# A routed mixture-of-experts layer behind attention: new opening and closing orders, and 18 idle products on TensorE

## The chip, the cores and the metric

The kernel runs on 1 core of one Trainium2 chip. The metric is device time in microseconds (us) of one launch. The engines are named as in the profile: PE is TensorE, DVE is VectorE, ACT is ScalarE, POOL is GpSimd, SP is the engine that issues most DMAs.

## The reference

Two residual blocks over x of shape (2, 1024, 128), in fp32:

```python
# attention with one latent for queries and keys
xn = layernorm(x)
latent = xn @ W_basis.T                        # 64 wide
v = xn @ W_v.T + b_v
scores = latent @ latent.T / sqrt(64)          # causal, within a batch
y = softmax(scores) @ v                        # same weights for all heads
x = x + layernorm(y @ W_o.T + b_o)
# 64 experts of 88 rows, top 8 of the best 4 of 8 groups, plus 2 shared ones
xn = layernorm(x)
s = sigmoid(xn @ gate_w.T); choice = s + gate_bias
group_score = sum of the two largest of each group of 8
masked = choice where the group is among the best 4, else 0
w = s at top8(masked); w = w / (sum(w) + 1e-20) * 2.5
routed = sum_e w[e] * (silu(xn @ Wg[e].T) * (xn @ Wu[e].T)) @ Wd[e].T
x = x + layernorm(routed + shared_mlp(xn))
```

## The kernel before

**Tiles.** The 2048 tokens are 16 tiles of 128 and four quarters ("quads") q of 512. Every expert product is one of 512 columns, and to keep fp32 accuracy each is done as three products of fp32r parts: high by high, high by low, low by high (`products`, lines 1303 to 1305). The weights of 16 experts by 8 rows make one chunk of 128 rows; there are 11 rounds of 4 chunks ("sets") c. A step is one chunk for one quad: gate and up (6 products), ACT's Silu (`gate`), DVE's up times route weight (`weigh`, line 1005) and gate times up (`hidden`, line 1015), ACT's high part (`hidden_hi`), POOL's low part (`hidden_lo`), and the down products (3) three steps later, which add up in one PSUM bank per quad.

**Order.** Each engine has its own program, and semaphores tie them. The steps of the first round and all of attention and routing are mixed by hand-written lists, `PE_ORDER`, `ACT_ORDER`, `DVE_ORDER` and `POOL_ORDER`; the last round and the output norm go by `PE_TAIL`, `ACT_TAIL`, `DVE_TAIL`, `POOL_TAIL`. Between them run plain loops over the rounds. An engine works through its list strictly in order: a stage that waits holds up all that stand behind it.

**Stages of the opening.** S statistics of x and P its norm and transposition (quad 0 on DVE, the others on POOL, `norm_x`); Q the latent product and its split into `lat_hi`, `lat_lo` and a scaled copy `lat_hl`; B on DVE the centring of W_o and b_o, B on POOL the making of `sel`, a matrix that copies a routing weight to its chunk's rows; K the product of W_v and W_o; V the values; A score rows and exponentials; T their transposition; C the weighted values; D, U, X, Y the attention's norm and the next one; E the transposed expert input, F the logits, H, J, I, O, M the routing (groups, experts, scores, sum of weights and `route`), G the transposition of `route`, N its spreading over the chunks (`route_w`), L and R the splits of shared and routed weights. Z is gate and up of a step, W its hidden parts and, on PE, the down products of the step two before.

Before anything else PE does ten products of 128x128 identities, and nothing reads them (line 1377).

**Stages of the closing.** D k is the down product of step k-3. The last quad is done in two halves of 256 columns. T k on PE multiplies finished columns by `center` (I - 1/128), which transposes them and takes their mean off; S k and N k on DVE are its statistics and the scaling and residual (line 1122), Y k the reciprocal root: on POOL for units 0 to 3, and for the last, unit 4, on ACT (Sqrt, line 839) with a DVE reciprocal. O copies a finished bank to `y_t`; O3 on ACT copies the last quad's bank, and O4 on DVE (line 1099) adds the second half's bank to it, after the last down products and ahead of T4. W20 on DVE makes the last low part.

Of the kernel before, what the change touches and what calls it, by code (L numbers as in the profile page):

```python
# [1499 lines left out]
```

## Time and profile before

| | |
|---|---|
| time, median of 3 runs | 477.61 us (476.32 to 477.9) |
| the profiled execution's own time | 477.6 us |
| its span, from the first to the last instruction | 475.6 us |
| PE busy | 455.8 us (96%) |
| DVE busy | 325.5 us (68%) |
| POOL busy | 335.9 us (71%) |
| ACT busy | 286.0 us (60%) |
| mean granted TensorE clock | 0.983 |

Busy times are modelled for PE, whose products overlap, so the spacing of their starts tells more than the duration of one. The granted clock is a share of full speed: 1.00 is 2.4 GHz, 0.50 is 1.2 GHz. All times in the rows count from the span's start.

### The profile page before, as it was taken

Reading aid. Unit: us, or ns where it says so; the run is one execution under the profiler, and the core shown is the slowest. Engines: PE = TensorE matmul, PEld = TensorE weight load, DVE = VectorE, ACT = ScalarE, POOL = GpSimd, SP = SyncE. Lnnn points to the kernel's source line nnn. Section 1 sums busy time; section 2 is a strip of 40 time slices with the busy share of each in tenths; the row PEclk is TensorE's granted clock in tenths of the full one; section 3 lists DMA queues with packets and bytes.
Section 4 is the critical chain, followed back from the end, with each engine's and each line's share of the span. In section 5 each row is a group of like instructions: output and inputs, shape, how many; then the busy total and the mean of one; then the engine's idle time right before and its main releaser. Section 6 shows DMA issues by size and latency. Waiting matters only on the chain.

```text
span 475.6 us, 8043 instructions
## 1 busy us (share of the span) xinstructions
PE 455.8 (96%) x2152; PEld 370.5 (78%) x2152; DVE 325.5 (68%) x694; ACT 286.0 (60%) x573; POOL 335.9 (71%) x318
## 2 busy tenths in 40 slices
PE   6999986999999999999999999999999999999995
PEld 4889774767778888888888888888888888888894
DVE  5666989786466666666666666666666666666786
ACT  2577985855665565565556555555655555566563
POOL 6853667765677767777776777777677777768674
PEclk8899997999999999999999999999999999999999
DMA  7000000000010100001010000101000010100002
GB/s 180 25 3 2 18 17 19 17 1 0 1 51 19 34 17 20 31 17 33 17 33 17 23 26 17 33 17 33 17 22 28 17 33 17 33 0 0 0 23 67
DMA packets 12856, 11.58 MB, mean 24 GB/s; under 512 B 2549, under 2 KB 12837, under 8 KB 12837
## 3 DMA queue, kind: packets, MB, share of 16 engines
q1 hardware_dynamic: 11973, 11.02, 8.0%
q10 hardware_dynamic: 864, 0.33, 0.4%
q8 instruction: 9, 0.15, 0.1%
q14 instruction: 10, 0.08, 0.1%
HBM read 10.30 MB, written 1.05 MB: 24 GB/s over the span
## 4 chain that ended last, share of the span: by engine, by line
PE 89%; ACT 5%; DVE 2%; issue 2%; DMA 1%; ACTq 0%; POOL 0%; DVEq 0%
PE ps L1303 27%; PE ps L1305 26%; PE ps L1304 26%; PE ps L1255 2%; PE ps L1243 1%; PE ps L1203 1%; PE ps L1274 1%; PE ps L1298 1%; PE ps L1195 1%; PE ps L1223 1%; PE ps L1224 1%; PE ps L1454 1%; DMA bv_sb<-in_b_v 1%; ACT xn L672 1%; ACT exp_t L712 1%
## 5 line engine op out<-in xcount | busy, mean ns | idle before, releaser
L547 POOL TENSOR_TENSOR lat_hi<-hid,lat_hl 128x512 fp32r<-128x512 f32 (+1 forms) x187 | 239.9, 1285 | 101.5 <-ACT lat_hl L768 97.1
L754 ACT ACTIVATE ps<-ps 128x512 f32<-128x512 f32 (+1 forms) x180 | 103.1, 573 | 132.1 <-PE ps L1305 131.8
L1005 DVE TENSOR_TENSOR up_w<-ps,route_w 128x512 f32<-128x512 f32 (+1 forms) x180 | 122.2, 679 | 85.2 <-PE ps L1305 84.7
L1015 DVE TENSOR_TENSOR hid<-ps,up_w 128x512 f32<-128x512 f32 (+1 forms) x180 | 122.4, 680 | 33.6 <-DVE up_w L1005 28.3
L1303 PE MATMUL ps<-x_hi,w_hi 128*128 128x512 f32 (+1 forms) x360 | 141.2, 392 | 2.8 <-ACT route_w L740 2.4
L1305 PE MATMUL ps<-x_hi,w_lo 128*128 128x512 f32 (+1 forms) x360 | 140.5, 390 | 0.0
L1304 PE MATMUL ps<-x_lo,w_hi 128*128 128x512 f32 (+1 forms) x360 | 140.2, 389 | 0.0
L768 ACT CAST lat_hl<-hid 128x512 fp32r<-128x512 f32 (+1 forms) x188 | 113.4, 605 | 14.2 <-DVE hid L1015 11.7
L1303 PEld LDWEIGHTS ps<-x_hi,w_hi 128*128 128x128 f32 x360 | 68.0, 189 | 19.4 <-issue 4.3
L1305 PEld LDWEIGHTS ps<-x_hi,w_lo 128*128 128x128 f32 x360 | 68.1, 189 | 15.0
L1304 PEld LDWEIGHTS ps<-x_lo,w_hi 128*128 128x128 f32 x360 | 68.0, 189 | 14.5
L1303 PE MATMUL ps<-lat_hl,w_hi 128*128 128x512 f32 (+1 forms) x180 | 71.4, 397 | 0.5 <-POOL lat_hi L547 0.5
L1305 PE MATMUL ps<-lat_hl,w_lo 128*128 128x512 f32 (+1 forms) x180 | 69.7, 387 | 0.0
L1304 PE MATMUL ps<-lat_hi,w_hi 128*128 128x512 f32 (+1 forms) x180 | 69.2, 385 | 0.0
L555 POOL TENSOR_TENSOR w_lo<-w_raw,w_hi 128x384 fp32r<-128x384 f32 x44 | 45.0, 1024 | 3.1 <-ACT w_hi L748 3.1
L1303 PEld LDWEIGHTS ps<-lat_hl,w_hi 128*128 128x128 f32 x180 | 33.8, 188 | 8.4 <-POOL lat_hi L547 1.2
L1305 PEld LDWEIGHTS ps<-lat_hl,w_lo 128*128 128x128 f32 x180 | 33.7, 187 | 8.1
L1304 PEld LDWEIGHTS ps<-lat_hi,w_hi 128*128 128x128 f32 x180 | 33.8, 188 | 7.2
L748 ACT CAST w_hi<-w_raw 128x384 fp32r<-128x384 f32 x44 | 22.6, 517 | 4.9 <-PE ps L1305 4.9
L895 DVE TENSOR_REDUCE neg_max<-ps 128x1 f32<-128x128 f32 (+7 forms) x16 | 12.0, 752 | 11.1 <-PE ps L1225 11.0
L1255 PE MATMUL ps<-vals,exp_t 128*128 128x129 f32 x144 | 18.3, 278 | 0.6 <-ACT att L693 0.4
L1255 PEld LDWEIGHTS ps<-vals,exp_t 128*128 128x128 f32 x144 | 17.1, 191 | 1.4 <-issue 1.2
(140 smaller groups left out, 366.9 us busy)
## 6 DMA issues: line engine op xcount, KB each, us to landing
w_raw<-in_w_experts SPq DMA_DIRECT2D x44, 192.0 KB, 2.4
x_sb<-in_x SPq DMA_DIRECT2D x3, 256.0 KB, 4.9
out<-x_sb SPq DMA_DIRECT2D x3, 256.0 KB, 2.3
x_sb<-in_x ACTq DMA_DIRECT2D x2, 64.0 KB, 2.3
x_sb<-in_x SPq DMA_DIRECT2D x2, 64.0 KB, 2.1
out<-x_sb SPq DMA_DIRECT2D x1, 128.0 KB, 1.8
out<-x_sb SPq DMA_DIRECT2D x2, 64.0 KB, 1.6
sh_raw<-in_w_shared_up SPq DMA_DIRECT2D x1, 88.0 KB
```

Of the source, the lines that this page charges most:

```text
L547: g.tensor_tensor(hid_lo[:, k % DEEP, 0:w], hid[:, k % 2, 0:w], hid_hi[:, k % DEEP, 0:w], ALU.subtract).then_inc(s_hlo, 1)
L555: g.tensor_tensor(w_lo[:, c, :], w_raw[:, c, :], w_hi[:, c, :], ALU.subtract).then_inc(s_wlo, 1)
L748: a.copy(w_hi[:, c, :], w_raw[:, c, :]).then_inc(s_whi, 1)
L754: a.activation(bank, bank, ACT.Silu).then_inc(s_gated, 1)
L768: a.copy(hid_hi[:, k % DEEP, 0:w], hid[:, k % 2, 0:w]).then_inc(s_hhi, 1)
L895: v.tensor_reduce(neg_max[:, k:k + 1], rows.rearrange("p a b -> p (a b)")[:, 0:width], AX.X, ALU.max, negate=True).then_inc(s_max, 1)
L1005: v.tensor_tensor(up_w[:, k % 2, 0:w], ps[:, gate_bank(k) + 1, 0:w], route_w[:, group, 512 * q + lo:512 * q + lo + w], ALU.mult).then_inc( ...
L1015: v.tensor_tensor(hid[:, k % 2, 0:w], ps[:, gate_bank(k), 0:w], up_w[:, k % 2, 0:w], ALU.mult).then_inc(s_hid, 1)
L1255: mm = t_.matmul(ps[:, 7, 256 * (r % 2):256 * (r % 2) + C + 1], exp_t[:, r % 2, j, :], vals[:, (q // QPB) * TPB + j, 0:C + 1], start=(j == 0),
L1303: t_.matmul(out_, hi, mhi, start=start, stop=False)
L1304: t_.matmul(out_, hi, mlo, start=False, stop=False)
L1305: return t_.matmul(out_, lo, mhi, start=False, stop=stop)
```

## The change

- **Opening norm.** The reciprocal root of quad 0 leaves POOL: ACT takes a Sqrt, DVE a reciprocal, and each normalised tile is signalled by itself. Two small activations (Sqrt, Exp) are placed to bring their tables in.
- **Latent.** `lat_hi` is signalled before its scaled copy, which is now read from `lat_hi`.
- **Routing weights.** One small DVE operation per quad is gone: the 2.5 stands in `sel`, the 1e-20 in a 65th column of `left`.
- **Idle products.** A stage I on PE: 2, 6 and 10 products of 512 columns into a bank that the next user overwrites. Line 1377's ten become eight, and one more follows P0.
- **Closing.** The down weights of the last chunk are centred beforehand (stage C: three DVE operations, one ACT copy, one POOL subtraction), and the last down product is done as six products of 128 columns that add to T4's bank; T3 and T4 stand before it. The last two units' variances come from ACT (Square with a running sum, then Sqrt), not from DVE's statistics and POOL's power.
- **Orders.** All eight lists are rewritten.
- **Buffers.** `wc` and `wc_hi` stand where `left` stood and are together as large; the other new ones and `left` stand behind all the rest. `deviation` is twice as long.

```diff
-        deviation = sb("deviation", [P, 4])
+        deviation = sb("deviation", [P, 2, 4])
-        left = sb("left", [P, 4, E])
+        wc = sb("wc", [P, C])
+        wc_hi = sb("wc_hi", [P, C], F32R)
...
+        first_dev = sb("first_dev", [P, 6])
+        y_var = sb("y_var", [P, 2, 2])
+        wc_stats = sb("wc_stats", [P, 6])
+        wc_mean = sb("wc_mean", [P, 2])
+        left = sb("left", [P, 4, E + 1])
+        wc_lo = sb("wc_lo", [P, C], F32R)
...
         PE_ORDER = stages(
-            "P0 Q0 K0 V0 A00 P1 A01 A02 Q1 T00 T02 A03 C00 C01 T04 T06 A10 C02 C03 A11 P2 V1 "
...
-            "E1 T34 F1 T35 W1 C31 G0 T36 T37 Z0 C32 N00 C33 Z1 E2 F2 Z2 N01 G1 Z3 W2 Z4 W3 Z5 "
+            "P0 Q0 K0 A00 V0 P1 A01 A02 T00 Q1 A03 T02 C00 C01 T04 T06 A10 C02 C03 A11 P2 T10 "
...
+            "E1 T34 F1 T35 C31 T36 G0 Z0 W0 T37 C32 N00 C33 Z1 E2 F2 N01 Z2 I0 G1 I1 Z3 W1 I2 "
+            "W2 Z4 W3 Z5 E3 W4 Z6 N10 F3 N11 W5 G2 Z7 W6 W7 N20 Z8 Z9 W8 W9 N21 Z10 Z11 Z12 "
...
         ACT_ORDER = stages(
-            "R2 T37 Z0 N00 Y2 C33 Z1 E2 R3 F2 G1 W0 N01 W1 Z2 W2 Z3 Z4 Y3 W3 Z5 W4 E3 Z6 W5 "
+            "G0 T36 T37 Y2 N00 C33 Z1 E2 F2 G1 Z2 N01 W0 W1 Z3 W2 R3 Y3 W3 Z4 Z5 W4 E3 Z6 W5 "
...
         DVE_ORDER = stages(
-            "S0 B0 P0 S1 S2 B1 Q0 A00 A01 A02 K0 V0 A03 Q1 S3 A10 A11 A12 V1 U0 A13 Q2 X0 V2 "
-            "A20 A21 Q3 A22 A23 U1 F0 A30 X1 V3 H0 A31 A32 J0 I0 O0 M0 A33 U2 F1 X2 H1 G0 J1 "
-            "Z0 I1 O1 Z1 U3 F2 M1 H2 J2 X3 Z2 I2 Z3 G1 Z4 O2 Z5 M2 Z6 F3 G2 Z7 H3 Z8 Z9 J3 Z10 "
+            "S0 P0 S1 B0 B1 Q0 K0 A00 V0 A01 A02 S2 A03 Q1 A10 S3 A11 A12 V1 A13 U0 Q2 A20 X0 "
+            "V2 A21 Q3 A22 A23 U1 V3 X1 A30 F0 A31 H0 A32 J0 I0 O0 U2 M0 A33 X2 F1 H1 G0 J1 Z0 "
+            "I1 O1 Z1 U3 M1 F2 H2 J2 X3 Z2 I2 Z3 G1 Z4 Z5 O2 M2 Z6 F3 G2 Z7 H3 Z8 Z9 J3 Z10 "
...
         POOL_ORDER = stages(
-            "S0 S1 P1 B0 S2 P2 D0 S3 P3 X0 D1 F0 X1 L0 J0 D2 E0 R0 M0 F1 R1 X2 E1 L1 J1 D3 E2 "
-            "F2 M1 W0 R2 J2 W1 X3 R3 W2 W3 W4 M2 F3 W5 W6 E3 W7 W8 J3 W9 W10 W11 W12 M3 W13 "
+            "B0 S1 P1 S2 P2 S3 D0 P3 X0 R0 D1 R1 R2 F0 X1 L0 L1 E0 J0 D2 M0 F1 X2 J1 E1 D3 F2 "
+            "M1 E2 J2 W0 X3 W1 R3 W2 W3 W4 E3 M2 W5 F3 W6 W7 W8 W9 J3 W10 W11 W12 M3 W13 W14 "
...
         PE_TAIL = stages(
-            "D11 Z13 D12 Z14 D13 Z15 D14 Z16 D15 Z17 T2 D16 D17 D18 Z18 T3 Z19 D19 D20 D21 D22 "
-            "T4 "
+            "D11 Z13 D12 Z14 D13 Z15 D14 Z16 Z17 D15 T2 Z18 D16 D17 D18 Z19 D19 D20 D21 T3 T4 "
+            "D22 "
...
         ACT_TAIL = stages(
-            "W11 Z11 Z12 W12 W13 Z13 Z14 W14 Z15 O2 Z16 W15 W16 Z17 O3 W17 W18 Z18 Z19 W19 W20 "
-            "Y4 P0 "
+            "O1 W11 Z11 Z12 W12 Z13 W13 Z14 W14 W15 Z15 O2 Z16 Z17 W16 W17 Z18 W18 W19 Z19 O3 "
+            "W20 Y3 Y4 P0 "
...
         DVE_TAIL = stages(
-            "Z19 W20 S3 O4 N2 S4 N3 N4 "
+            "S2 Z19 O4 W20 N2 N3 N4 "
...
+        FILLS = (2, 6, 10, )
...
                     link(g.affine_select(out=sel_f[:], in_=sel_f[:], compare_op=ALU.not_equal,
-                                         fill=1.0, base=base, channel_multiplier=1,
+                                         fill=ROUTED_SCALE, base=base, channel_multiplier=1,
...
+                elif what == "C":
+                    pool.wait_ge(s_wchi, 1)
+                    g.tensor_tensor(wc_lo[:], wc[:], wc_hi[:], ALU.subtract).then_inc(s_wclo, 1)
...
-            a.copy(lat_hi[:, own], ps[:, 1, :])
-            a.activation(lat_hl[0:R, own], ps[0:R, 1, :], ACT.Identity,
-                         scale=SCALE).then_inc(s_lhi, 1)
+            a.copy(lat_hi[:, own], ps[:, 1, :]).then_inc(s_lhi, 1)
+            act.wait_ge(s_lhi, q + 1)
+            a.activation(lat_hl[0:R, own], lat_hi[0:R, own], ACT.Identity,
+                         scale=SCALE).then_inc(s_lhs, 1)
...
             for n in range(2, 4):
                 a.dma_start(x_sb[:, n, :], x_tiles[:, n, :]).then_inc(s_x0[n], 16)
+            act.wait_ge(s_eps, 1)
+            a.activation(first_dev[:, 4:5], eps_col[:], ACT.Sqrt)
             a.dma_start(wv_sb[:], w_v).then_inc(s_wvl, 16)
             a.dma_start(wo_sb[:], w_o_t).then_inc(s_wvl, 16)
             a.dma_start(bv_sb[:], b_v).then_inc(s_wvl, 16)
             a.dma_start(bo_sb[:], b_o.to_broadcast([P, C])).then_inc(s_bol, 16)
+            act.wait_ge(s_var, 1)
+            a.activation(first_dev[:, 0:4], mv[:, 0, :, 1], ACT.Sqrt,
+                         bias=eps_col[:]).then_inc(s_dev0, 1)
+            a.activation(first_dev[:, 5:6], eps_col[:], ACT.Exp)
...
                 elif what == "Y":
-                    act.wait_ge(s_var, len(VARIANCES) + k + 1)
-                    a.activation(deviation[:, 0:2], mv[:, 2 + k % 2, 0:2, 1], ACT.Sqrt,
+                    act.wait_ge(s_yp, k + 1)
+                    for t in range(UNITS[k][2]):
+                        ins = a.activation(squares[:, t, 0:C], ps[:, unit_bank(k), P * t:P * t + P],
+                                           ACT.Square, scale=float(C) ** -0.5,
+                                           accum_out=y_var[:, k % 2, t:t + 1])
+                    ins.then_inc(s_yvar, 1)
+                    act.wait_ge(s_yvar, k - len(UNITS) + 3)
+                    a.activation(deviation[:, k % 2, 0:2], y_var[:, k % 2], ACT.Sqrt,
                                  bias=eps_col[:]).then_inc(s_dev, 1)
...
+            def norm_x0():
+                dve.wait_ge(s_dev0, 1)
+                v.reciprocal(rstd[:, 0], first_dev[:, 0:4]).then_inc(s_rstd, 1)
+                dve.wait_ge(s_rstd, 1)
+                for t in range(4):
+                    ins = v.tensor_scalar(xn[:, 0, t, :], x_sb[:, t, :], mv[:, 0, t, 0:1],
+                                          rstd[:, 0, t:t + 1], ALU.subtract, ALU.mult)
+                    ins.then_inc(s_xn0, 1)
...
                 link(v.tensor_reduce(wsum[:], left[:], AX.X, ALU.add))
-                link(v.tensor_scalar(wsum[:], wsum[:], 1e-20, 1.0 / ROUTED_SCALE, ALU.add,
-                                     ALU.mult))
                 v.reciprocal(winv[:], wsum[:]).then_inc(s_winv, 1)
...
+                elif what == "C":
+
+                    dve.wait_ge(s_wl[SETS - 1], 16 * ROUNDS)
+                    rows = w_raw[:, SETS - 1, WD:WD + P]
+                    link(v.bn_stats(wc_stats[:], rows))
+                    link(v.bn_aggr(wc_mean[:], wc_stats[:]))
+                    v.tensor_scalar(wc[:], rows, wc_mean[:, 0:1], None,
+                                    ALU.subtract).then_inc(s_wc, 1)
                 elif what == "O":
 
-                    dve.wait_ge(s_down, LAST_S + unit_step(k) + 1)
+                    dve.wait_ge(s_down, LAST_S + unit_step(k))
...
+                pe.wait_ge(s_lhs, q + 1)
                 pe.wait_ge(s_llo, q + 1)
...
+            def last_down(k):
+
+                pe.wait_ge(s_wclo, 1)
+                pe.wait_ge(s_hlast, 1)
+                for t in range(2):
+                    own = slice(P * t, P * t + P)
+                    to = ps[:, unit_bank(len(UNITS) - 1), own]
+                    hi, lo = hid_hi[:, k % DEEP, own], hid_lo[:, k % DEEP, own]
+                    t_.matmul(to, hi, wc_hi[:], start=False, stop=False, skip_group_check=True)
+                    t_.matmul(to, hi, wc_lo[:], start=False, stop=False, skip_group_check=True)
+                    mm = t_.matmul(to, lo, wc_hi[:], start=False, stop=True,
+                                   skip_group_check=True)
+                mm.then_inc(s_yp, 1)
+
+            def fill_wait(k):
+
+                pe.wait_ge(s_eta, turns_through(4 * QUADS))
+                for _ in range(FILLS[k]):
+                    t_.matmul(ps[:, acc_bank(0), :], ident_r[:], x_hi[:, 0:512], start=True, stop=True)
...
-            for _ in range(10):
-                t_.matmul(ps[:, 6, 0:P], ident[:], ident[:], start=True, stop=True)
+            def keep_busy(n):
+                for _ in range(n):
+                    t_.matmul(ps[:, 6, 0:P], ident[:], ident[:], start=True, stop=True)
+
+            keep_busy(8)
             for at, (what, q, n) in enumerate(PE_ORDER):
                 if what == "P":
                     turn_xn(q, at)
+                    if q == 0:
+                        keep_busy(1)
```

## Rows read from the trace of the kernel before

**Rows 1.** Busy time in stretches: us, each engine's busy us (instructions), granted clock, DMA.
```profile
0.00:66.54 66.54, 59.73 (x400) 51.83 (x400) 46.44 (x182) 46.77 (x120) 40.17 (x67) 0.95 0.17 44
66.54:81.00 14.46, 9.01 (x35) 6.92 (x36) 12.57 (x54) 7.29 (x18) 10.15 (x11) 0.76 0.06 15
74.00:88.00 14.00, 11.64 (x42) 8.69 (x43) 13.09 (x49) 10.26 (x21) 10.89 (x13) 0.76 0.10 29
...
110.00:430.00 320.00, 319.31 (x1382) 257.81 (x1381) 210.87 (x306) 188.04 (x349) 234.03 (x192) 1.00 0.08 22
```

**Rows 2.** Whom TensorE waited for, 64 to 120: us, times, longest.
```profile
PE ps L1303 <- ACT route_w L740: 2.4, 1, 2.4
PE ps L1283 <- POOL route L575: 1.7, 1, 1.7
```

**Rows 3.** The same busy-time columns in half microseconds, around the clock's falls and rises.
```profile
9.00:9.50 0.50, 0.47 (x1) 0.32 (x2) 0.47 (x3) 0.00 (x0) 0.42 (x2) 0.75 0.97 217
...
16.00:16.50 0.50, 0.50 (x5) 0.50 (x4) 0.20 (x1) 0.50 (x2) 0.50 (x1) 0.92 0.00 0
...
74.00:74.50 0.50, 0.00 (x0) 0.00 (x0) 0.48 (x1) 0.50 (x2) 0.00 (x0) 0.60 0.00 0
...
80.50:81.00 0.50, 0.50 (x2) 0.36 (x2) 0.50 (x1) 0.00 (x0) 0.35 (x2) 0.57 0.00 0
```

**Rows 4.** Chain that ended last, one piece at low clock: start, us, what.
```profile
77.84 0.43 PE ps L1303
```

**Rows 5.** Timeline of the opening: start, us, engine, line, operation [idle before].
```profile
3.64 1.28 ACT L659 ACT_TABLE_LOAD   x1 [3.64 <-issue]
3.97 0.38 DVE L867 BATCH_NORM_AGGREGATE mv<-stats 128x2 f32<-128x6 f32 x4
...
5.78 0.29 DVE L987 BATCH_NORM_STATS2 wo_stats<-wo_sb 128x6 f32<-128x128 f32 x1 [1.44 <-DMA bv_sb<-in_b_v]
...
6.53 1.11 DVE L876 TENSOR_SCALAR xn<-x_sb,mv,rstd 128x128 f32<-128x128 f32 x4
...
9.03 1.89 PE L1195 MATMUL ps<-xn_t,wb_sb 128*128 128x512 f32 x2 [0.68 <-ACT xn_t L659]
...
10.46 3.41 POOL L565 TENSOR_SCALAR xn<-x_sb,mv,rstd 128x128 f32<-128x128 f32 x4
...
12.32 2.05 PE L1203 MATMUL ps<-wvo_sb,xn_t 128*128 128x128 f32 x8 [0.55 <-ACT wvo_sb L783]
```

**Rows 6.** Timeline from the second quarter's routing to the first routed step.
```profile
71.28 0.48 DVE L979 TENSOR_SCALAR wsum<-wsum 128x4 f32<-128x4 f32 x1
...
72.04 1.04 POOL L575 TENSOR_TENSOR route<-left,winv 128x512 f32<-128x512 f32 x1 [0.32 <-DVE winv L981]
...
74.89 1.08 ACT L740 COPY route_w<-ps 128x512 f32<-128x512 f32 x2
...
81.08 0.69 DVE L1015 TENSOR_TENSOR hid<-ps,up_w 128x512 f32<-128x512 f32 x1
```

**Rows 7.** Timeline of the last ten microseconds.
```profile
465.31 0.59 ACT L843 COPY y_t<-ps 128x512 f32<-128x512 f32 x1 [1.92 <-PE ps L1305]
...
468.81 1.28 ACT L839 ACT_TABLE_LOAD   x1
468.83 0.42 DVE L1105 TENSOR_TENSOR lat_hi<-hid,lat_hl 128x256 fp32r<-128x256 f32 x1 [0.47 <-ACT lat_hl L768]
...
469.97 0.42 DVE L1099 TENSOR_TENSOR y_t<-ps,y_t 128x256 f32<-128x256 f32 x1
...
470.45 0.71 PE L1454 MATMUL ps<-center,y_t 128*128 128x128 f32 x4 [0.52 <-DVE y_t L1099]
...
472.15 0.30 ACT L839 ACTIVATE deviation<-mv,eps_col 128x2 f32<-128x2 f32 x1 [2.05 <-DVE mv L867]
...
472.75 0.61 DVE L1122 SCALAR_TENSOR_TENSOR x_sb<-ps,rstd,x_sb 128x128 f32<-128x128 f32 x2
```

**Rows 8.** Instructions of line 690: ns min/median/max, first and last start.
```profile
L690 ACT ACTIVATE squares<-ps x16: 271/280/287, 20.7 to 66.5; 128x129 f32<-128x129 f32 x16
```

More of the change, by code:

```diff
@@ L318, in stage_before @@
             return found[-1] if found else None
-        NORMS = [st[:2] for st in POOL_ORDER if st[0] in "SDX"]
+        NORMS = [("S", 0)] + [st[:2] for st in POOL_ORDER if st[0] in "SDX"]
         VARIANCES = [st[:2] for st in DVE_ORDER if st[0] in "SX"]
@@ L483, in _ @@
             g.memset(minus_half[:], -0.5)
+            g.memset(left[:, :, E:E + 1], 1e-20)
             g.memset(eps_col[:], EPS).then_inc(s_eps, 1)
@@ L574, in write_route @@
                     pool.wait_ge(s_rtp, q)
-                g.tensor_tensor(route[:], left[:].unsqueeze(2).to_broadcast([P, 4, 2, E]),
+                g.tensor_tensor(route[:], left[:, :, 0:E].unsqueeze(2).to_broadcast([P, 4, 2, E]),
                                 winv[:, :].unsqueeze(2).unsqueeze(3).to_broadcast([P, 4, 2, E]),
@@ L835, in _ @@
                     act.wait_ge(s_eps, 1)
-                    a.activation(deviation[:, 2:3], eps_col[:], ACT.Sqrt)
+                    a.activation(deviation[:, 0, 2:3], eps_col[:], ACT.Sqrt)
                 elif what == "Y":
-                    act.wait_ge(s_var, len(VARIANCES) + k + 1)
-                    a.activation(deviation[:, 0:2], mv[:, 2 + k % 2, 0:2, 1], ACT.Sqrt,
+                    act.wait_ge(s_yp, k + 1)
[6 more added lines that the diff above has]
+                    a.activation(deviation[:, k % 2, 0:2], y_var[:, k % 2], ACT.Sqrt,
                                  bias=eps_col[:]).then_inc(s_dev, 1)
+                elif what == "C":
+                    act.wait_ge(s_wc, 1)
+                    a.copy(wc_hi[:], wc[:]).then_inc(s_wchi, 1)
                 elif what == "O":
@@ L870, in _ @@
             made = [0]
-            def scale(n, k, src, dst):
-                dve.wait_ge(s_rstd, n + 1)
-                for t in range(4):
-                    ins = v.tensor_scalar(dst(t), src(t), mv[:, k, t, 0:1], rstd[:, k, t:t + 1],
-                                          ALU.subtract, ALU.mult)
-                return ins
             def flat(t3):
@@ L965, in choose_experts @@
                 for t in range(4):
-                    ins = v.match_replace(left[:, t, :], top8[:, t, :], masked[:, t, :], TAKEN)
+                    ins = v.match_replace(left[:, t, 0:E], top8[:, t, :], masked[:, t, :], TAKEN)
                 link(ins)
@@ L972, in pick_scores @@
                     dve.wait_ge(s_route, q)
-                v.scalar_tensor_tensor(out=left[:], in0=left[:], scalar=TAKEN, in1=scores[:, q % 2],
-                                       op0=ALU.is_equal, op1=ALU.mult).then_inc(s_picked, 1)
+                v.scalar_tensor_tensor(out=left[:, :, 0:E], in0=left[:, :, 0:E], scalar=TAKEN,
+                                       in1=scores[:, q % 2], op0=ALU.is_equal, op1=ALU.mult).then_inc(s_picked, 1)
             def sum_weights(q):
@@ L1114, in _ @@
                     q, first, n = UNITS[k]
-                    if k + 1 == len(UNITS):
+                    if k + 2 >= len(UNITS):
                         dve.wait_ge(s_rstd, len(NORMS) + k)
-                        dve.wait_ge(s_dev, 1)
-                        v.reciprocal(rstd[:, 2 + k % 2, 0:n], deviation[:, 0:n]).then_inc(s_rstd, 1)
+                        dve.wait_ge(s_dev, k - len(UNITS) + 3)
+                        v.reciprocal(rstd[:, 2 + k % 2, 0:n],
+                                     deviation[:, k % 2, 0:n]).then_inc(s_rstd, 1)
                     dve.wait_ge(s_rstd, len(NORMS) + k + 1)
@@ L1404, in _ @@
                     logits(q, at)
+                elif what == "I":
+                    fill_wait(q)
                 elif what == "Z":
@@ L1443, in _ @@
                         down(kd, LAST_S + kd, q, w_hi[:, c, :], w_lo[:, c, :], P,
-                             start=(lo > 0 and c == 0), stop=(c == SETS - 1), lo=lo, w=w)
+                             start=(lo > 0 and c == 0),
+                             stop=(c == SETS - (2 if lo else 1)), lo=lo, w=w)
                 elif what == "T":
@@ L1455, in _ @@
                                        y_t[:, q, P * (first + t):P * (first + t) + P], center[:],
-                                       start=True, stop=True, skip_group_check=True)
-                    mm.then_inc(s_yp, 1)
+                                       start=k + 1 < len(UNITS) or t == 0, stop=True,
+                                       skip_group_check=True)
+                    if k + 1 < len(UNITS):
+                        mm.then_inc(s_yp, 1)
 def kernel(L0_attn_hidden_states, L0_attn_W_basis, L0_attn_W_v, L0_attn_b_v, L0_attn_W_o,
```

42 lines of the change are left out of this document (26 added, 16 removed), and 23 rows, old and new, of tables (ACT_ORDER, DVE_ORDER, PE_ORDER, POOL_ORDER).

## The prediction

> **What bounds the kernel now.** I read the page's shares first: PE 96% busy, DVE 68%, POOL 71%. That is a mean, so the next view is the busy time by stretches [rows 1]. From 110 to 430 us, PE is busy for 319.3 of 320 us with 1382 products, one every 0.231 us: the loops are PE's, and no edit touches them. What can be won lies in the 110 us before and the last 12 us. The reader is to see there three kinds of loss.
>
> First, PE stands still or starts late in the opening: the first latent product starts at 9.03 us [rows 5]. Second, between 66.5 and 81 us PE is busy for only 9.0 of 14.5 us [rows 1]; the view of who waited for whom puts 1.7 us on POOL's `route` and 2.4 us on ACT's `route_w` [rows 2]. Third, the granted clock: it falls at 9.25 us and is back at 16.0, and falls at 74.1 and is back at 80.9 (the shares 0.75, 0.92, 0.60 and 0.57 of half-microsecond windows give the points) [rows 3]. Both stretches last 6.8 us at 0.50, which is 1.2 GHz. Before each, PE had been doing short work with gaps. In the second a product takes 0.43 us instead of 0.231 [rows 4]. PE works in it from 76.2 (its wait ends just behind the copies at 75.97 [rows 6]) to 80.9, so 4.7 us of time did what takes half: 2.35 us lost, at most.
>
> At the end, PE's last products end at 471.16 us and the span at 475.6: a chain of statistics, root, scaling and a DMA.
>
> **The opening.** Before: statistics ready at 3.97 + 0.38 = 4.35; DVE then waits for the weights (until 5.76) for the centring, and norms only at 6.53 to 7.64; PE transposes from 7.70, ACT copies, and the latent product starts at 9.03 [rows 5]. Now P0 stands ahead of the centring. ACT has issued its last DMA at 3.6. The new Sqrt table load comes right behind the first two DMA issues. If it lies beside the other four, Sqrt runs at 4.4, 0.30 long [rows 7], the reciprocal ends at about 4.9, and the tiles are ready by 6.05 (1.11 as in [rows 5]). Eight idle products end there too. Transposition ends near 6.5, the copy 0.6 later, the latent product starts at 7.2: 1.8 us earlier. If the load holds the issues up by its 1.28 us plus an activation, all is 0.5 later (gain 1.3) and W_o, the value weights and b_o land 1.5 us later. DVE's Q0 now stands behind B1, which waits for b_o; that can eat another 0.7 or so. The Exp load, 1.28 [rows 5], lies from 4.7 to 6.0, under the norm. It costs nothing while the transposition ends after 6.1, and up to 0.5 us when it doesn't.
>
> What follows? V0 ran from 12.32 to 14.37, with A00 and P1 behind it [rows 5], so P1 came no earlier than 14.7. Now A00 goes as soon as the split is done, near 10.1, and V0 behind it. P1 needs POOL's norm of quad 1 (3.41 long, ending at 13.87 [rows 5]). POOL makes `sel` first now and then starts it when DVE's statistics, which stand behind P0, are there: 7.3 + 1.5 + 3.4 = 12.2. So PE idles a little before P1 again, and the gain there is 14.7 - 12.3 = 2.4 at most. If the clock falls as before, V0 costs 2.05 again [rows 5] and P1 comes 1 us earlier or less. From 16 to 66 us PE is nearly gapless and ACT runs close to full in places, so what is won is carried but not increased. I take 1.8 us; bounds 0.3 (issues late, clock fallen, b_o late) and 3.5 (no low stretch over dense work: half of 1.89 and of 2.05 back, plus the earlier start).
>
> The two loads here are priced by the profile: 1.28 us each, at both places where one is seen [rows 5, 7]. What the trace cannot show is the rest of a switch, because both of its loads end in a long wait. The Trainium skill (ScalarE: Activation LUTs, section What ACT_TABLE_LOAD costs) gives 2.66 us for every switch of set, a drain being part of it; by that the opening's sum would be 1.0 us instead of 1.8, an estimate from that page. I go by the trace, and the dearer switch is a rival below.
>
> **The middle.** The DVE operation that is gone took 0.48 us for quad 1 [rows 6]. M1 is also moved ahead of F2 on DVE. On POOL, F2 still stands ahead of M1, but E2 (x's low part) now comes behind M1. `route` started at 72.04 and would start at 71.45, 0.6 earlier; so does G1 on PE. Z3 doesn't wait for G1 itself. It waits for ACT's two `route_w` copies (1.08 us [rows 6]), which stand behind G1 on ACT, and now behind Z2's Silu too, which I price as ACT's copy of 512 columns, 0.59 [rows 7]; of the 0.6 little is left if PE is late with it, but Z2's product is long done. So Z3, which waited until the copies ended at 75.97, starts some 0.5 us earlier, near 75.7 against 76.2: the waits stay. Into them go the idle products: 2 before G1 (0.46 us; in a wait that was 1.7 us and is now 1.1), 6 before Z3 (1.39, in one that was 2.4 [rows 2]), and 10 before the first down product (2.31). PE's longest pause shrinks from 2.4 to about 1.2 us, so I expect the second low stretch to be gone, +2.35 us.
>
> The last ten are covered only in part. The down product needs POOL's low part of step 0, which needs ACT's W0, now behind N01, and on POOL stands behind E2 and J2: about 78.3. Z3 at full clock ends at 77.1 and the ten at 79.4: 1.1 us too many. Without their cover all ten would cost 2.3.
>
> And PE cannot cash in everything: DVE is busy for 13.09 of the 14 us from 74 to 88 [rows 1], with routing and step work mixed. Z5 needs step 3's `hidden`, which ended at 81.77 [rows 6], 0.8 us after the clock was back. DVE has 0.9 us of idle time in those 14 us, and gains the removed operation, 0.48; so with DVE behind it PE can come about 1.4 us earlier. The sum by PE is 0.5 + 2.35 - 1.1 = 1.75. I take 1.5 us, between the two; bounds -1 (fills late, DVE order worse) and 3.5.
>
> **The closing.** ACT's O3 waited 1.92 us for the last quad's down products [rows 7] with two high parts queued behind it; these delay POOL, and so steps 18 and 19. Now O3 stands behind Z19, and Z18 stands three down products earlier (1.05 us). W20's part on DVE started at 468.83; its input would be there near 467.6 by the 1.05 us and what O3 no longer holds up. Then O3 (0.59), O4 (0.42) and the low part (0.42) follow on ACT and DVE: about 468.6. PE: T3 behind D21 and O3, T4 behind O4, end near 468.7; last product, six of 128 columns, about 0.65: 469.4.
>
> Then the price. ACT's Y3 does two squares (0.28 each [rows 8]; with their sums read I take 0.75 for two, up from 0.56), and only then needs Sqrt's table. Before, the load ran at 468.81, hidden in a wait of 2 us [rows 7]. Now it stands between Y3's squares and its root, and Y4 queues behind it: 468.25 + 0.75 + 1.28 + 0.3 = 470.6, squares to 471.35, root 471.7, reciprocal 471.9, scaling 0.61: 472.5 against 473.36 [rows 7]. Gain 0.8 us; bounds -0.6 (the shortening above fails, the load stays) and 2.1 (the load is hidden). Stage C adds 0.8 us to DVE, 0.3 to ACT and 0.4 to POOL in a stretch where PE is the bound; two DVE statistics and one POOL root go. I cost it at nothing; if DVE were late there, 0.8.
>
> **The sum.** 1.8 + 1.5 + 0.8 = 4.1 us. The profiled execution took 477.6 us with 2.0 outside its span, and its time is the median of the runs shown. So 477.6 - 4.1 = 473.5 us.
>
> **Rivals.**
> (a) *Half of it is lost on the way* (0.14): the opening's low stretch only moves. It stays as long, but now lies over denser work, from 12.7 to 19.5 instead of 9.3 to 16.1. For: the new opening leaves PE idle around 9.1 to 10.1 and before 12.2. Price: 1 to 2 us more; with DVE holding the middle to 0.5, the time is 475.6 to 476.8.
> (b) *More than summed* (0.19): no low stretch in the opening once PE works, and the middle gains by DVE's lighter queue: 3.3 + 2.7 + 1.0, 470.6 us.
> (c) *The idle products don't hold the clock* (0.10): it falls before Z3 anyway. They then run at 0.43 us each: six take 2.56 against about 2.5 of wait, but ten take 4.3, and in the kernel before the down product followed Z3 without a wait. That is +4.3 on PE's path with the 2.35 not won: 477.6 + 4.3 - 1.8 - 0.8 = 479.3, slower. It decides as soon as the clock is at half when I2 begins. Against: PE's idle share before is halved.
> (d) *Nothing measurable* (0.05): fills and waits cancel, 477 us.
> (e) *A table switch costs twice its load* (0.04): ACT stands for another 1.28 us after each [rows 5, 7]. In the opening 0.8 of that shows, at the end all of it: 473.5 + 0.8 + 1.3 = 475.6. For: no load in this trace is followed at once by work. The drain of the page named above is such a mechanism.
>
> **How the numbers follow.** The forecast case (472 to 475.5) has 0.48. 0.3% (1.4 us) is what a measurement of this kernel can tell from no change, so faster is below 476.2: 0.48, (b), (e) and half of (a), 0.78. Same: the rest of (a) and (d), 0.12. Slower: (c), 0.10. The range takes in (b), (e) and all of (a): 470.5 to 477.0; that leaves (c), and the outer ends of (b) and (d), out.
>
> **What would show it.** Latent product at 7.2 to 7.8; P1 near 12.3 to 13.5; a granted clock of 1.00 from 70 to 85 us; the ten idle products before the first down product beginning near 77; Z5 some 3 us ahead of its old 82.9; an ACT table load between Y3's squares and Sqrt; loops with one product every 0.231 us as before. The prediction is wrong if a low stretch lies over the first routed steps, if PE waits longer for DVE between 80 and 118, or if the opening's gain is gone by 66.

## The result, and the profile after

The changed kernel takes 473.94 us (median; before 476.32 in the same series), a ratio of 0.9954, 95% interval 0.9941 to 0.9966: faster by 0.46%, 2.2 us (2.4 us between the medians). The forecast was 473.5 us, but as a gain of 4.1 us from 477.6; some two fifths of that gain are missing. Most executions of one kernel fall into two groups some 1.4 us apart (after: 473.75 to 473.94, and 475.13 to 475.50, with a single one of 1147.85 us far outside both), and both profiled executions, 477.6 us before and 475.2 us after, are of the longer group; the section on the hardware says what differs.

To see where the time went I took the same piece of work in both traces and read when PE starts it. Before, in the timeline of PE (start, us, engine, line): the first product of E2, the last spreading of route weights N31, and T2.

```profile
66.54 0.63 PE L1265 MATMUL ps<-ident,xn 128*128 128x128 f32 x4 [0.24 <-ACT xn L672]
...
118.21 0.47 PE L1298 MATMUL ps<-route_t,sel 128*128 128x512 f32 x1 [0.28 <-DVE hid L1015]
...
463.17 0.27 PE L1454 MATMUL ps<-center,y_t 128*128 128x128 f32 x1
```

The same three in the timeline of the changed kernel:

```profile
66.83 0.27 PE L1312 MATMUL ps<-ident,xn 128*128 128x128 f32 x1
...
116.95 0.70 PE L1345 MATMUL ps<-route_t,sel 128*128 128x512 f32 x2 [0.28 <-DVE hid L1046]
...
461.83 0.27 PE L1528 MATMUL ps<-center,y_t 128*128 128x128 f32 x1
```

| stretch | before | after | gain | forecast |
|---|---|---|---|---|
| start to E2 | 66.54 | 66.83 | -0.29 | 1.8 |
| E2 to N31 | 51.67 | 50.12 | 1.55 | 1.5 |
| N31 to T2 (the loops) | 344.96 | 344.88 | 0.08 | 0 |
| T2 to the span's end | 12.43 | 11.47 | 0.96 | 0.8 |
| span | 475.6 | 473.3 | 2.3 | 4.1 |

The whole miss lies ahead of E2. The stretches of the changed kernel (us, busy us of PE, PE's weight loads, DVE, ACT, POOL, then granted clock, DMA share and GB/s) stand against [rows 1, 3]:

```profile
66.83:82.00 15.17, 12.57 (x60) 9.53 (x59) 12.80 (x55) 8.62 (x18) 9.58 (x12) 1.00 0.00 1
110.00:430.00 320.00, 319.32 (x1378) 257.50 (x1377) 210.07 (x305) 187.40 (x349) 234.97 (x192) 1.00 0.08 22
...
13.50:14.00 0.50, 0.32 (x2) 0.35 (x3) 0.16 (x1) 0.00 (x0) 0.04 (x1) 0.76 0.00 0
17.00:17.50 0.50, 0.50 (x3) 0.26 (x1) 0.48 (x3) 0.00 (x0) 0.00 (x0) 0.82 0.00 0
```

The low stretch over the routing is gone (1.00 where 0.76 stood), and of the one in the opening 3.4 us are left, from about 13.8 to 17.2. The loops are as before. The waits of PE from 64 to 120 us (total, times, longest), against [rows 2], have shrunk as forecast:

```profile
PE ps L1350 <- ACT route_w L761: 1.0, 1, 1.0
PE ps L1330 <- POOL route L592: 0.4, 1, 0.4
```

The opening's timeline, against [rows 5]:

```profile
1.66 1.28 ACT L794 ACT_TABLE_LOAD   x1 [1.66 <-PEq L1569]
...
3.11 0.49 ACTq L798 DMA_DIRECT2D bo_sb<-in_b_o  x1
...
4.73 1.28 ACT L802 ACT_TABLE_LOAD   x1
4.75 2.32 POOL L518 TENSOR_SCALAR_AFFINE_SELECT sel_f<-sel_f 128x512 f32<-128x512 f32 x2
...
4.96 2.36 DVE L932 TENSOR_SCALAR xn<-x_sb,mv,rstd 128x128 f32<-128x128 f32 x4
...
8.39 1.13 PE L1241 MATMUL ps<-xn_t,wb_sb 128*128 128x512 f32 x2 [0.45 <-ACT xn_t L679]
...
10.16 3.38 POOL L582 TENSOR_SCALAR xn<-x_sb,mv,rstd 128x128 f32<-128x128 f32 x4
...
13.68 1.04 PE L1205 MATMUL ps<-ident,xn 128*128 128x128 f32 x4 [0.75 <-POOL xn L582]
```

The first load lies beside the DMA issues and holds none of them up. But DVE's four tiles take 2.36 us where they took 1.11, while POOL's two selections, 4.75 to 7.07, run beside them, and the statistics of quad 1 queue behind them. The latent product starts at 8.39, not at 7.2. POOL's norm of quad 1 starts at 10.16 (before 10.46), not at 8.8.

### The profile page after: what moved, and what is told of

Read it like the earlier page. It is cut to its first block, busy times and chain, and to the rows that moved or that the text cites. A ratio compares the mean times of both kernels' runs of the same rounds, so it can differ in the third digit from the quotient of the medians.

```text
span 473.3 us, 8089 instructions
## 1 busy us (share of the span) xinstructions
PE 455.9 (96%) x2171; PEld 371.6 (79%) x2171; DVE 325.9 (69%) x687; ACT 290.5 (61%) x587; POOL 333.2 (70%) x316
## 4 chain that ended last, share of the span: by engine, by line
PE 84%; POOL 5%; DVE 4%; issue 3%; ACT 1%; DMA 0%; DVEq 0%; SPq 0%; POOLq 0%; ACTq 0%
PE ps L1350 26%; PE ps L1352 25%; PE ps L1351 25%; PE ps L1302 2%; POOL lat_hi L564 1%; PE ps L1290 1%; POOL xn L582 1%; PE ps L1528 1%; POOL rstd L541 1%; PE ps L1241 1%; DVE hid L1046 1%; PE ps L1345 1%; PE ps L1270 1%; PE ps L1271 0%; POOL x_lo L529 0%
## 5 line engine op out<-in xcount | busy, mean ns | idle before, releaser
L1350 PEld LDWEIGHTS ps<-x_hi,w_hi 128*128 128x128 f32 x360 | 67.5, 188 | 19.1 <-issue 3.5
L1302 PEld LDWEIGHTS ps<-vals,exp_t 128*128 128x128 f32 x144 | 17.2, 192 | 1.5 <-issue 0.9
```

Of the source, the lines that this page charges most:

```text
L1302: mm = t_.matmul(ps[:, 7, 256 * (r % 2):256 * (r % 2) + C + 1], exp_t[:, r % 2, j, :], vals[:, (q // QPB) * TPB + j, 0:C + 1], start=(j == 0),
L1350: t_.matmul(out_, hi, mhi, start=start, stop=False)
```

## The experiments

Each kernel was timed in five rounds beside the kernel before. "E2 to N31" and "T2 to end" are the stretches of the table above, in the profiled execution. Order lists are shown as short extracts.

### The idle products taken out, and put alone into the kernel before

```diff
-        FILLS = (2, 6, 10, )
+        FILLS = (0, 0, 0, )
```

> The changed kernel with no idle product in the three stages I (the opening's nine stay). Theory, idle products hold the clock: TensorE stands still for longer than in the changed kernel before the first routed step, the granted clock falls there for one stretch (3.4 or 6.8 us), and half of that shows; the ten last ones give back at most 0.8 us of cover. Time 474.5 to 475.5 us against 473.9 of the changed kernel, loops' start (the last two products that spread quad 3's weights) 0.6 to 1.6 us later than 116.95. Rival, they are worth nothing, since VectorE with routing and step work sets the pace there: within 0.5 us of 473.9. Second rival, they stand in the way: 0.8 us faster, 473.1, with the first down product at 78.2 and not 78.98.

Measured: 474.42 us, ratio 0.9946 (0.9925 to 0.9967), which the interval doesn't tell from the changed kernel's 0.9954; the median is 0.5 us higher, but E2 to N31 takes 50.17 us against 50.12. The low stretch is back, from 74.4 to 81.2, and so is PE's wait for `route_w`. In its windows, waits and timeline of DVE:

```profile
74.00:81.00 7.00, 5.22 (x12) 3.69 (x13) 6.38 (x42) 4.29 (x9) 4.01 (x7) 0.53 0.00 0
...
PE ps L1350 <- ACT route_w L761: 2.4, 1, 2.4
...
81.96 0.69 DVE L1046 TENSOR_TENSOR hid<-ps,up_w 128x512 f32<-128x512 f32 x1 [0.46 <-POOL lat_hi L564]
```

The second half of the changed kernel's middle shows why it costs nothing:

```profile
75.18 0.47 PE L1350 MATMUL ps<-x_hi,w_hi 128*128 128x512 f32 x1 [0.96 <-ACT route_w L761]
...
76.65 2.49 PE L1399 MATMUL ps<-x_hi,ident_r 128*128 128x512 f32 x10
...
76.88 1.30 POOL L564 TENSOR_TENSOR lat_hi<-hid,lat_hl 128x512 fp32r<-128x512 f32 x1
...
78.98 0.39 PE L1350 MATMUL ps<-lat_hl,sh_hi 128*128 128x512 f32 x1
...
81.61 0.69 DVE L1046 TENSOR_TENSOR hid<-ps,up_w 128x512 f32<-128x512 f32 x1 [0.47 <-POOL lat_hi L564]
```

With the idle products step 3's `hidden` starts 14.78 us after E2 (81.61 - 66.83); without them 14.72 (81.96 - 67.24). PE at half clock is slower, but the chain over DVE and POOL is not, and PE waits for it either way. The chain that ended last, followed back, says the same: in the changed kernel it runs over POOL, DVE and ACT from 66 to 95 us, with two pieces of it here (start, us, what), and without the idle products it has the same pieces at 80.58 and 81.96.

```profile
80.22 1.26 POOL lat_hi L564
81.61 0.70 DVE hid L1046
```

For the same reason the ten products cost nothing though they overshoot: POOL's low part is done at 78.18 and the down product starts at 78.98, 0.8 us later.

The counterpart: the kernel before, its orders unchanged but for stage I.

```diff
-            "... E2 F2 Z2 N01 G1 Z3 W2 Z4 ..."
+            "... E2 F2 Z2 N01 I0 G1 I1 Z3 I2 W2 Z4 ..."
```

> The kernel before with nothing added but the three stages of idle products (2 ahead of G1, 6 behind it, 10 ahead of the first down product). Theory after the first runs, VectorE and GpSimd set the pace there: the granted clock stays at full through 74 to 81 us, and still the stretch from the third expert input's transposition (E2) to the last spreading product (N31) stays at 51.7 us within 0.4, the time at the 476.4 of the kernel before within 0.5. Rival, the clock matters where the orders are the old ones, since there 2.35 us of products ran at half clock: 474 to 475.5. Second rival, in the old order the first down product followed at once, so the ten cost their 2.3 us: 478.5.

Measured: 476.26 us, ratio 0.9999 (0.9984 to 1.0015). E2 to N31 takes 51.44 us against 51.67. The clock is held at full through the routing:

```profile
74.00:81.00 7.00, 6.30 (x27) 4.92 (x28) 6.73 (x30) 3.47 (x8) 6.66 (x10) 1.00 0.11 30
```

DVE is busy for 6.73 of these 7 us, POOL for 6.66. So the 18 idle products do what they are for, and together with what they cost they are worth nothing that can be measured, in either kernel (the interval here leaves room for 0.7 us either way).

The reason isn't shown to be the same in both. In the kernel before, the chain that ended last runs over PE alone from 76.22 to 91.45, half-clock products among it ([rows 4] is one of them), and in this run over PE from 74.70 to 89.67, with the ten idle products in it:

```profile
76.33 2.33 PE ps L1343 x10
```

They stand where POOL's low part has long been done (74.82), and the first down product starts 13.48 us after E2 instead of 12.38. So the idle products' own 2.33 us may have eaten what the clock gave back. Against that, the `hidden` of steps 2, 3 and 4 start at the same distance from E2 with and without them (17.03 us for step 4 in both), and only step 5's comes 0.5 earlier. Fewer idle products in the old order, which would part the two readings, were not tried.

This run also has the old opening without a low stretch, unlike the profile of before. Its timeline (PE and POOL):

```profile
9.10 1.13 PE L1197 MATMUL ps<-xn_t,wb_sb 128*128 128x512 f32 x2 [0.67 <-ACT xn_t L661]
...
10.37 3.22 POOL L567 TENSOR_SCALAR xn<-x_sb,mv,rstd 128x128 f32<-128x128 f32 x4
...
13.74 0.63 PE L1161 MATMUL ps<-ident,xn 128*128 128x128 f32 x4 [0.46 <-POOL xn L567]
...
65.01 0.63 PE L1267 MATMUL ps<-ident,xn 128*128 128x128 f32 x4 [0.23 <-ACT xn L674]
```

### The old closing

The closing lists, the last down product, T4 and the statistics of before, in the changed kernel:

```diff
-            "... Z17 D15 T2 Z18 D16 D17 D18 Z19 D19 D20 D21 T3 T4 D22 "
+            "... D15 Z17 T2 D16 D17 D18 Z18 T3 Z19 D19 D20 D21 D22 T4 "
```

> The changed kernel with the closing of the kernel before: its four closing lists, the last down product as before and T4 behind it, VectorE's statistics for the last two units. The opening and the middle stay. Theory, the closing gives its own gain behind a bound that only passes time through: 0.9 us slower than the changed kernel, 474.8. Rival, the closing only looks shorter because of where the execution stood (chance of the clock): within 0.3 us of 473.9. Third, the closing is all of the change: 476.3, no different from the kernel before.

Measured: 474.89 us, ratio 0.9958 (0.9942 to 0.9974), 0.95 us over the changed kernel; T2 to end takes 12.45 us again. The closing is worth 0.95 us by the medians and as much by the trace (12.45 against 11.5). The profiled execution had no low stretch in the opening, and E2 starts at 65.29.

### `sel` made after quad 1's norm

```diff
-            "B0 S1 P1 S2 P2 S3 D0 P3 X0 ..."
+            "S1 P1 B0 S2 P2 S3 D0 P3 X0 ..."
```

> The changed kernel with GpSimd's making of the selection matrix moved back behind its norm of quad 1, as before the change. One order only. Theory: VectorE's four normalisations of quad 0 took 2.36 us instead of 1.11 because GpSimd worked through the selection matrix beside them; they will take 1.1 us again, the first latent product starts near 7.2 us instead of 8.39, and quad 1's norm ends about 1.2 us earlier (12.3). Rival on the cause: the normalisations are slow for another reason (signalling each tile), and stay at 2.3 us. For the whole time: if the opening's lead is lost before 66 us anyway, no change within 0.3 us of 473.9; if it is carried, 472.7 to 473.3.

Measured: 472.75 us, ratio 0.9917 (0.9896 to 0.9938), 1.2 us under the changed kernel. Nothing stands beside DVE's tiles now (timelines of DVE, POOL and PE):

```profile
5.03 1.11 DVE L932 TENSOR_SCALAR xn<-x_sb,mv,rstd 128x128 f32<-128x128 f32 x4
...
6.35 1.06 PE L1205 MATMUL ps<-ident,xn 128*128 128x128 f32 x4
...
8.09 1.48 PE L1241 MATMUL ps<-xn_t,wb_sb 128*128 128x512 f32 x2 [0.25 <-ACT xn_t L679]
...
8.99 3.31 POOL L582 TENSOR_SCALAR xn<-x_sb,mv,rstd 128x128 f32<-128x128 f32 x4
...
12.82 0.60 PE L1205 MATMUL ps<-ident,xn 128*128 128x128 f32 x4
...
64.42 0.60 PE L1312 MATMUL ps<-ident,xn 128*128 128x128 f32 x4
```

The tiles take 1.11 us and are ready at 6.14, as forecast; POOL's norm starts 1.17 us earlier, P1 0.86 us earlier. The latent product gains only 0.3 us of the 1.2 that it was late: the transposition waits for the eight idle products until 6.35 and takes 1.06 us, where the kernel before took 0.66 (at 7.70) and the run below with both orders and no idle products in the middle, whose opening is the same, 0.65. Against the run with the old closing, whose opening has no low stretch either, E2 comes 0.87 us earlier (65.29 - 64.42): a lead at P1 is carried through the attention to the end. It isn't eaten by waits on the way, so the changed kernel never had a lead at P1.

### The last attention row's maximum ahead of the norm

```diff
-            "... J0 I0 O0 U2 M0 A33 X2 ..."
+            "... J0 I0 O0 M0 A33 U2 X2 ..."
```

> The changed kernel with VectorE's last row maximum (A33) ahead of the sum of attention and input for quad 2 (U2), as before the change; the order of the two is all that differs. Theory: TensorE's wait of 0.97 us at 59.35 for ACT's last exponentials comes from this order; the wait goes, the third expert input's transposition starts near 66.0 instead of 66.83, and 0.5 to 1.0 us of it reach the end: 472.9 to 473.4. Rival: what is won there is lost at the next link, since the sum for quad 2 is late and with it statistics and norm of quad 2, or ACT is full between 60 and 67: same time within 0.3 us, wait moved to another line.

Measured: 473.57 us, ratio 0.9927 (0.9908 to 0.9946), 0.4 us under the changed kernel, with intervals that overlap. There, U2's 1.13 us on DVE stand ahead of A33's maximum, and the waits of PE show what is late next:

```profile
PE ps L1290 <- ACT exp_rows L723: 1.2, 2, 1.0
```

Here the same two waits are, from 20 to 70 us:

```profile
PE ps L1290 <- ACT exp_rows L723: 0.4, 2, 0.2
```

0.8 us less wait gives 0.4 us from P2 to E2 (42.5 against 42.9), less than the 0.5 to 1.0 expected. The traced execution is one of 476.51 us, 3 us over the median, so only stretches inside it are compared; the section on the hardware comes back to it.

### Both of these, with the idle products, without them, and with six opening products

> The changed kernel with both orders restored: GpSimd's selection matrix behind its norm of quad 1, VectorE's last row maximum ahead of the sum for quad 2. Alone they measured 472.75 and 473.57 against 473.94. If the two are links in one row and each passes its time on: 472.3 to 472.4. If the second's 0.4 us is only an earlier arrival at the same wait: 472.75 again.

> As the run with both orders, and with no idle product in the three stages I. Theory, they are worth nothing at any lead of TensorE that these orders give: same as with them within 0.4 us, though the granted clock falls again near 75 us. Rival, with the lead larger, TensorE's half clock comes to the surface: 0.5 to 1.5 us slower than with them.

```diff
-            keep_busy(8)
+            keep_busy(6)
```

> The version with both orders restored (472.35), and with six idle products before the first transposition in place of eight. Theory: in the opening the eight end at 6.35 us and the first tiles are ready at 5.4 and all four by 6.1, so the transposition waits for idle products; with six it ends 0.4 to 0.5 us earlier and the time is 471.8 to 472.0. Rival: with fewer idle products the clock comes up later or falls again in the opening more often, and the time is the same or up to 1.5 us longer in part of the executions.

Measured: 472.35 us (0.9902, 0.9885 to 0.992) with both orders; 472.66 (0.9922, 0.9898 to 0.9945) with FILLS at zero, a low stretch from about 71.3 to 78.1 and E2 to N31 50.5 us against 50.2; 472.09 (0.9904, 0.9873 to 0.9935) with both orders and six opening products. The two orders add up (1.2 and 0.4 gave 1.6). The idle products are worth at most 0.3 us even here, which the intervals don't tell from nothing, and the same holds for the difference between eight and six, though the trace with six fits its 0.3: transposition from 5.51, latent product at 7.24, E2 at 63.56 against 63.81. The last of these is the best version: 1.0% under the kernel before, 0.4% under the changed one.

### The middle, one edit at a time

The old order of the routing on DVE and POOL; the small DVE operation on `wsum` put back; the scores' pick O2 earlier; the old order of spreading on PE and ACT:

```diff
-  DVE "... U3 M1 F2 H2 ..."        POOL "... D3 F2 M1 E2 J2 ..."
+  DVE "... U3 F2 M1 H2 ..."        POOL "... D3 E2 F2 M1 J2 ..."
```

> The changed kernel with the order of quad 1's routing as before the change: on VectorE the sum of the weights (M1) behind the sigmoid (F2), on GpSimd the low part of quad 2's input (E2) ahead of the bias and of route (F2, M1). The removed operation stays removed. Theory: route of quad 1 starts 0.6 us or more later again, Z3 with it, and 0.6 to 1.2 us of the 1.5 us that the middle won are lost: 474.5 to 475.1. Rival: TensorE and ScalarE's order (the second spreading products ahead of step 2, Silu ahead of the copies) won it, and this changes nothing: 473.9 within 0.3.

```diff
-                                         fill=ROUTED_SCALE, base=base, channel_multiplier=1,
+                                         fill=1.0, base=base, channel_multiplier=1,
...
+                link(v.tensor_scalar(wsum[:], wsum[:], 0.0, 1.0 / ROUTED_SCALE, ALU.add,
+                                     ALU.mult))
```

> The changed kernel with the small VectorE operation on the sum of the weights back in each of the four quads (the 2.5 taken out of the selection matrix again). Theory, the removed operation pays where VectorE sets the pace, in quads 1 to 3: 0.3 to 0.5 us of the middle's 1.5 us go, 474.2 to 474.5. Rival, it lies beside waits: within 0.2 us of 473.9, and the stretch from E2 to the last spreading product stays at 50.2 us.

```diff
-  DVE "... Z3 G1 Z4 Z5 O2 M2 Z6 ..."
+  DVE "... Z3 G1 Z4 O2 Z5 M2 Z6 ..."
```

> The changed kernel with VectorE's picking of quad 2's scores (O2) ahead of step 5's work again, as before the change, and not behind it. Theory: this operation, 1.1 to 1.6 us when GpSimd works beside it, holds up step 5, on which TensorE's steps 6 and 7 wait; the third stage E comes 0.4 to 0.7 us later against E2, and 0.5 to 1.0 us reach the end: 474.4 to 474.9. Rival: TensorE has lead enough there; within 0.3 us of 473.9.

```diff
-  PE "... E2 F2 N01 Z2 I0 G1 ..."      ACT "... E2 F2 G1 Z2 N01 W0 W1 Z3 ..."
+  PE "... E2 F2 Z2 N01 I0 G1 ..."      ACT "... E2 F2 G1 W0 N01 W1 Z2 Z3 ..."
```

> The changed kernel with two orders as before the change around the second spreading products of quad 0: on TensorE they stand behind step 2 again and not ahead of it, and on ScalarE the high part of step 0 and the copies of route_w stand ahead of step 2's Silu. Theory: Silu of step 2 comes later and with it VectorE's step 2, the start of the row of steps that sets the pace; 0.5 to 1.0 us slower, 474.4 to 474.9. Rival: step 3's wait for the copies decides, and these come at the same time or earlier: within 0.3 us of 473.9 or up to 0.5 us faster.

| edit to the changed kernel | us | ratio (95%) | E2 to N31 |
|---|---|---|---|
| none | 473.94 | 0.9954 (0.9941 to 0.9966) | 50.1 |
| old routing order | 473.94 | 0.995 (0.993 to 0.997) | 50.2 |
| `wsum` operation back | 475.43 | 0.9972 (0.9952 to 0.9991) | 50.8 |
| O2 ahead of Z5 | 474.07 | 0.9949 (0.9926 to 0.9971) | 50.4 |
| old spreading order | 473.9 | 0.994 (0.9916 to 0.9964) | 50.1 |

Only the removed operation shows. The median with it back lies between six executions of 474.61 to 474.78 us and six of 476.07 or more; the shorter six lie 0.8 us over the changed kernel's 473.75 to 473.94, and the trace gives 0.7 (50.8 - 50.1), more than the 0.3 to 0.5 expected. In its timeline one of the three is:

```profile
86.28 0.67 DVE L1012 TENSOR_SCALAR wsum<-wsum 128x4 f32<-128x4 f32 x1
```

It lasts 0.67 us while POOL's split of x (85.45, 1.47 us) runs beside it, and 0.17 us in the two other places. The three orders, each by itself, are worth nothing that shows: at most 0.3 us between E2 and N31 and 0.1 in the medians.

## Why the prediction was right, and where not

**The opening failed: forecast 1.8, measured -0.3.** The step that failed is "the tiles are ready by 6.05 (1.11 as in [rows 5])". The rest of that step held: the table loads were hidden, Sqrt ran at 4.42, the reciprocal ended at 4.93, and nothing was delayed behind the DMA issues. But in [rows 5] the four tiles were scaled while POOL stood, and I had myself put POOL's making of `sel` over the new place. It made them 1.25 us longer and, through DVE's statistics queued behind them, POOL's norm of quad 1 later. `sel` moved away gives 1.2 us back. Two smaller sizes behind it were off as well. "Eight idle products end there too" (6.05) measured 6.35, and "Transposition ends near 6.5" measured 7.4 with the tiles in time, so the latent product still started at 8.09 and not at 7.2; six idle products gave 7.24. The forecast's own sign, the opening's gain gone by 66, came true.

The second part of the miss is the base. [rows 3, 5] show P1 and V0 under a low clock; where there is none, the old opening starts P1 at 13.74 and the new one at 13.71 (the run with the old routing order), because POOL's norm ends at 13.59 in the one and at about 13.56 in the other. E2 is then at 65.01 and 65.35. So "2.4 at most" for P1 was measured against a low stretch that comparable executions don't have, and the real gain at P1 was nothing. The sentence that PE is nearly gapless from 16 to 66 us, so that the lead is carried, is right for the orders of before and missed one of the new ones: A33's maximum behind U2, 0.4 us.

**The middle: forecast 1.5, measured 1.55, by luck and for another reason.** The idle products held the clock at 1.00, began at 76.65 (forecast near 77) and overshot by 0.8 (forecast 1.1); Z3 started at 75.18 (forecast 75.7); Z5 started at 82.56, only 0.4 us ahead of its old place (82.92) where "some 3 us" was forecast for the whole kernel, and 0.65 us nearer to E2. The "+2.35 us" for the clock is the wrong term: net of the idle products' own time it measured at 0.0 to 0.3 (50.17 against 50.12; 51.67 against 51.44; 50.5 against 50.2). In the changed kernel DVE and POOL set the pace there. I had the row for that, DVE busy for 13.09 of 14 us [rows 1], and used it as a cap of 1.4 instead of asking what PE's term was worth under it. What was taken for the small part, the removed operation, gives 0.7 of the 1.55. The idle products alone gave 0.2 in the kernel before. Another 0.6 is the difference between 51.44 (old orders, full clock) and 50.8 (new orders with the operation back); none of the three orders tried carries it alone. It may be in their sum, or in the places of W0, W5, Y3 and R3, or in E2's part on POOL, which weren't tried one by one. It may also be the ten idle products, which the old order leaves uncovered on PE and the new one covers for the most part. That stays open.

**The closing: forecast 0.8, measured 0.95.** The mechanism is the one forecast, and the run with the old closing confirms its worth. The last ten microseconds after, against [rows 7]:

```profile
465.33 0.60 ACT L879 COPY y_t<-ps 128x512 f32<-128x512 f32 x1
...
466.49 1.39 PE L1528 MATMUL ps<-center,y_t 128*128 128x128 f32 x8
...
467.77 1.28 ACT L872 ACT_TABLE_LOAD   x1
...
468.22 0.28 PE L1391 MATMUL ps<-wc_hi,lat_hi 128*128 128x128 f32 x1
...
469.07 0.29 ACT L872 ACTIVATE deviation<-y_var,eps_col 128x2 f32<-128x2 f32 x1
...
470.51 0.61 DVE L1165 SCALAR_TENSOR_TENSOR x_sb<-ps,rstd,x_sb 128x128 f32<-128x128 f32 x2
```

O3 no longer waits, and the load stands between Y3's squares and its root, as forecast. Two sizes are off against each other. From T2 the last product ends 6.67 us on (468.50 - 461.83) instead of 7.99 (471.16 - 463.17): 1.3 us won, where 1.8 was forecast (471.16 - 469.4). And from the end of PE's last product to the end of the last scaling it takes 0.4 us longer than before (2.62 against 2.20), with the load in it, instead of 0.9: the load starts 0.73 us before PE has ended, where the forecast had 0.4. That the two misses nearly cancel is luck.

**The rivals.** "Half of it is lost on the way" came near, counted as a gain: its 475.6 is 2.0 us off 477.6, and 2.4 were measured. In the profiled execution the low stretch did move over denser work (13.8 to 17.2), at half its length; but the run with the old routing order, which has none, shows the opening's gain missing all the same. It also speaks against "More than summed", which asked for such an opening. "The idle products don't hold the clock" is refuted by the clock of 1.00 over the routing in the changed kernel and in the kernel before with them. "A table switch costs twice its load" is refuted: Sqrt starts 0.02 us after the load's end (467.77 + 1.28 = 469.05 against 469.07), and the small Exp of the opening as well (4.73 + 1.28 = 6.01 against 6.03). The Trainium skill (ScalarE: Activation LUTs, section What ACT_TABLE_LOAD costs) gives 2.66 us for a switch, a load of about 1283 ns and a drain of about 1380; the load agrees with the 1.28 us here, and no drain shows, so the measurement decides. The forecast time of 473.5 came out close partly by luck, because the base moved: 4.1 us off 477.6 and 2.4 us off 476.32 end 0.4 us apart.

## What to carry to other kernels

Before work is put beside another engine's, look whether the duration that you carry over was measured beside idle neighbours: in these traces a DVE operation was two to five times as long while POOL worked. Before you buy TensorE's clock, ask which engine sets the pace in that stretch, and set what the idle products take on PE against what the clock gives. And take the base from an execution near the median, above all where one stretch of it is at low clock.

## What the runs showed of the hardware

- **DVE beside POOL.** Four 128x128 `tensor_scalar` take 1.11 us alone and 2.36 beside POOL's selections; a 128x4 operation 0.17 and 0.67. Not every operation pays: in the changed kernel `hidden`, which reads PSUM and SBUF, never takes more than 0.693 us in 180 times (line 1046), though the one at 200.15, for example, lies beside POOL's `hidden_lo` (199.75 to 201.06). One kernel's own instructions of one line range as widely, here line 969 of the changed kernel (ns min/median/max):

```profile
L969 DVE TENSOR_TENSOR low<-choice x4: 277/284/1361, 47.8 to 92.1; 128x128 f32<-128x128 f32 x4
```

- **The clock in the opening differs between kernels and executions.** The profiled execution of before has a low stretch of 6.8 us there, the changed kernel's one of 3.4; the kernel with `sel` late, the one with the old closing and the one with idle products alone have none once the clock is up. E2 stands 1.5 us later in before than in the kernel with idle products alone (66.54 against 65.01), with the same opening: about what separates the two groups of executions. Which of them an execution joins is not explained by these runs.
- **The clock column is no proof at the start.** The trace of the run with the last row's maximum first (476.51 us) shows this in PE's timeline and in a window:

```profile
8.58 2.07 PE L1241 MATMUL ps<-xn_t,wb_sb 128*128 128x512 f32 x2 [0.25 <-ACT xn_t L679]
...
13.30 2.02 PE L1249 MATMUL ps<-wvo_sb,xn_t 128*128 128x128 f32 x8
...
13.00:13.50 0.50, 0.50 (x4) 0.50 (x4) 0.00 (x0) 0.00 (x0) 0.41 (x1) 1.00 0.05 18
```

The column says 1.00, but the same products take 1.13 and 1.11 us in the changed kernel's trace, and 1.89 and 2.05 in the low stretch of before [rows 5]. So PE ran at half speed there. The trace's first clock entry, a rise to 1.00, comes at 19.1 us in this run, and at 6.9 in the changed kernel's; ahead of it the column shows 1.00 without an entry. In the other runs it comes between 5.7 and 8.8; with `sel` late it is 8.8, and the transposition at 6.35 took 1.06 us, while the same opening with the entry at 6.4 took 0.65. The run with the old spreading order (476.97 us) is another such case, with E2 at 68.62. In the opening, the durations of PE's products tell the clock, not the column.
